# PE's order from a shorter figure for the tops' rows, expert weights stored by SyncE, and x1's low part one unit earlier, in a fused attention and expert kernel on one core

## What is computed

```python
masked = (qb >= kb) & (idx[None, :] - idx[:, None] - 2 * (kb - qb) >= 1)      # chunks of 64
scores = jnp.einsum('bqhd,bkhd->bhqk', q, k) * attn_scale[0]                  # 16 heads of 8
attn = jax.nn.softmax(jnp.where(mask[None, None], -jnp.inf, scores), axis=-1)
x = _layernorm(x + out @ Wo.T + bo)

scores = jax.nn.sigmoid(logits)                     # 32 experts in 8 groups, per token
# 4 best groups, in them 6 best experts, weights normed and times 2.5: combine[T, E]
for each expert: routed += combine[:, e] * ((silu(x @ g.T) * (x @ u.T)) @ dn.T)
shared_out = (silu(x @ shared_gate_w.T) * (x @ shared_up_w.T)) @ shared_down_w.T
x = _layernorm(x + routed + shared_out)
```

## Time and profile before

| | |
|---|---|
| time, median of 3 runs | 441.92 us (441.58 to 442.02) |
| profiled execution | 443.63 us, its span 441.6 us |
| PE busy | 411.4 us, 93% of the span |
| VectorE busy | 343.4 us, 78% |
| ScalarE busy | 226.8 us, 51% |
| GpSimd busy | 134.9 us, 31% |
| TensorE's granted clock, mean | 0.948 |

### The profile page before, as it was taken

One profiled execution on the slowest core, in us unless ns is written; L12 is line 12 of the kernel. 1 busy time (PEld: TensorE's weight loads), 2 busy tenths in 40 slices (PEclk: granted clock), 3 DMA queues, 4 the chain that ended last, 5 costly groups with the idle time before them and its releaser, 6 DMA issues.

```text
span 441.6 us, 8102 instructions
## 1 busy us (share of the span) xinstructions
PE 411.4 (93%) x2870; PEld 216.7 (49%) x2870; DVE 343.4 (78%) x775; ACT 226.8 (51%) x309; POOL 134.9 (31%) x257
## 2 busy tenths in 40 slices
PE   5659999999999999999989989999999999999993
PEld 2424434343333334334334446766776776666661
DVE  4969988898989898989954564976778768778863
ACT  4610077775778696877777784232432253332220
POOL 5000236685575666566554250000000000000000
PEclk9955579999999999999999998999999999999997
DMA  4565141120303012020000007333222233334430
GB/s 122 187 206 162 41 125 53 33 81 7 106 4 88 27 40 74 25 76 6 3 3 4 1 29 122 107 115 96 91 92 105 92 105 95 126 95 128 135 95 24
DMA packets 27391, 34.51 MB, mean 78 GB/s; under 512 B 5912, under 2 KB 16472, under 8 KB 27352
## 3 DMA queue, kind: packets, MB, share of 16 engines
q1 hardware_dynamic: 27016, 33.34, 25.6%
q10 hardware_dynamic: 336, 0.66, 0.5%
HBM read 29.33 MB, written 4.65 MB: 77 GB/s over the span
## 4 chain that ended last, share of the span: by engine, by line
PE 79%; DVE 13%; ACT 3%; issue 2%; DMA 1%; ACTq 1%; SPq 0%; POOL 0%; DVEq 0%; POOLq 0%
PE ps L1248 16%; PE ps L1350 13%; PE ps L1205 11%; DVE mx L907 10%; PE ps L1318 7%; PE ps L1320 7%; PE ps L1319 7%; PE ps L1229 7%; PE ps L1209 3%; ACT probs L805 2%; PE ps L1271 2%; PE ps L1283 1%; ACTq L542 1%; DMA bk<-in_bk 1%; PE ps L1171 1%
## 5 line engine op out<-in xcount | busy, mean ns | idle before, releaser
L907 DVE TENSOR_REDUCE mx<-ps 128x1 f32<-128x512 f32 (+3 forms) x304 | 179.5, 656 | 23.2 <-PE ps L1209 19.2
L805 ACT ACTIVATE probs<-ps 128x1024 f32<-128x1024 f32 (+2 forms) x160 | 143.4, 940 | 51.6 <-PE ps L1229 51.1
L1205 PE MATMUL ps<-rows_k,rows_q 48*128 48x512 bf16 (+3 forms) x384 | 103.0, 361 | 11.2 <-DMA rows_k<-scratch 7.1
L847 ACT ACTIVATE rows_q<-ps 128x512 f32<-128x512 f32 x68 | 40.6, 599 | 93.3 <-PE ps L1320 92.5
L1248 PE MATMUL ps<-probs,Vg 128*32 128x512 f32 (+3 forms) x768 | 82.5, 502 | 0.3 <-POOL probs L705 0.3
L1229 PE MATMUL ps<-rows_q,rows_k 51*128 51x512 bf16 (+3 forms) x384 | 71.5, 334 | 2.7 <-ACT probs L805 2.1
L1318 PE MATMUL ps<-x1hi,w_hi 128*128 128x512 f32 x136 | 73.9, 543 | 0.1
L1129 DVE TENSOR_TENSOR rows_k<-ps,rows_q 128x512 f32<-128x512 f32 x64 | 43.9, 686 | 34.5 <-PE ps L1350 34.1
L1205 PEld LDWEIGHTS ps<-rows_k,rows_q 48*128 48x128 bf16 x384 | 30.1, 96 | 80.8 <-DVE mx L907 65.0
L1350 PE MATMUL ps<-rows_q,w_down 128*128 128x512 f32 x136 | 69.7, 594 | 0.0
L701 POOL TENSOR_SCALAR_AFFINE_SELECT probs<-probs 64x512 f32<-64x512 f32 x64 | 42.3, 661 | 77.9 <-ACT probs L805 76.8
(11 more groups left out here) (107 smaller groups left out, 332.9 us busy)
## 6 DMA issues: line engine op xcount, KB each, us to landing
comb_rows<-weights SPq DMA_DIRECT2D x128, 128.0 KB, 3.0
scratch<-oT SPq DMA_DIRECT2D x8, 384.0 KB, 3.3
w_raw<-in_unitT SPq DMA_DIRECT2D x17, 128.0 KB, 2.4
rows_q<-scratch SPq DMA_DIRECT2D x16, 96.0 KB
rows_k<-scratch SPq DMA_DIRECT2D x14, 96.0 KB
w_down<-in_unitT SPq DMA_DIRECT2D x1, 1088.0 KB, 5.9
xT<-in_xT SPq DMA_DIRECT2D x4, 256.0 KB, 4.4
rows_q<-scratch SPq DMA_DIRECT2D x16, 64.0 KB
```

Source lines behind the costliest of these rows:

```text
L805: act.activation(dst, src, ACT.Exp).then_inc(exps_ready, 1)
L907: dve.tensor_reduce(dst, src, AX.X, ALU.max).then_inc(max_read, 1)
L1205: mm = pe.matmul(bank(max_bank(k), m, at), q, rows_k[r0:r0 + ROWS_QK, s, j * T + k0:j * T + k0 + m], start=True, stop=not first, tile_posi ...
```

## The change

Three edits.
1. The figure for the rows of a top in the planner goes from 6500 to 4700 ns. This alone changes `pe_order`, and with it `act_order` and `pool_order`.
2. The weights by expert: the planner's due time of ScalarE's copy loses 1500 ns, which puts the copy of the first chunk ahead of the last exponential in `act_order`. The store of each chunk (and the wait ahead of it) moves from ScalarE to SyncE, in front of the loads that read it.
3. VectorE's low part of x1 for the second quad stands behind unit 0 and not behind unit 1.

```diff
-    hop, rows_latency, load = 240, 6500, 7500
+    hop, rows_latency, load = 240, 4700, 7500
@@ attention_order
-                act_todo.append(("t", 0, i[k], t + hop + (1500 if kind == "comb" else 0), 500))
+                act_todo.append(("t", 0, i[k], t + hop, 500))
@@ SyncE's program
             for n in range(NC):
+                cols = slice(n * BANK, (n + 1) * BANK)
+                wait_step(sp, (n // 2, "comb", n % 2, 0))
+                sp.dma_start(a["weights"][:, cols], combT[:, cols]).then_inc(comb_stored[n], 16)
                 sp.wait_ge(comb_stored[n], 16)
@@ ScalarE's program, tail_step
                     act.copy(combT[:, cols], src[0:E, :]).then_inc(o, 1)
-                    act.wait_ge(o, count)
-                    act.dma_start(a["weights"][:, cols], combT[:, cols]).then_inc(comb_stored[n], 16)
@@ VectorE's program, the loop over units
-                if i == 1:
+                if i == 0:
                     x1_low((0, "x1T", 1, 0))
```

## The result

The changed kernel takes 443.64 us (median of 10 runs, 442.08 to 444.21) against 441.37 us (10 runs, 441.06 to 442.02) for the kernel before on the same chip. The ratio is 1.0042, with a 95% interval of 1.0029 to 1.0055: 0.4% slower. The prediction was 439.4 us and faster; it was wrong in the sign, and the time lies above its range. The profiled execution took 444.08 us, its span is 442.3.

The account below looks back on a forecast made before the run. The prediction took TensorE's time as the kernel's time, held up differently by stage. Its terms, -1.04 - 1.15 - 0.35 = -2.54 us off the median of 441.92, gave 439.4 us, with a range of 436.9 to 442.4.

Parts of the forecast that it names:

- part 1, pause: Ahead of the logits of x1's second quad: moving the low part removes TensorE's whole standstill, -1.04 us.
- part 1, low clock: At 269 to 273 us: without the standstill TensorE's clock no longer falls, -1.15 us, with 0 as other bound.
- part 2: Weights by expert: earlier copy on ScalarE, stores issued by SyncE, cost 0, up to +0.5 us if cover is gone.
- order, start: First scores come 1.3 us earlier and the clock rises as much earlier: -0.65 us (0 to -1.3).
- order, middle: Regular head groups: one more place where TensorE waits for a maximum, +0.1 us a group, +0.5 over five.
- order, end: Behind the last maximum: two score units and one value product fewer are left, -0.2 us.
- Part 1: x1's low part behind unit 0: TensorE's standstill and the low clock both go, -2.2 us together.
- rival D: End of attention: last maximum later, VectorE's chain holds TensorE before the transposes, clock falls; +1.4 us, 443.3, chance 0.12.
- Rival E: x1's low part finds its high part late, the standstill only moves; -0.35 us is left, 441.6, chance 0.05.
- rival C: Middle: new order loses 0.5 us in each of five groups, +2.5; -0.54 in all, 441.4, chance 0.13.

Follow-up runs that it names:

- before_a: The kernel before, unchanged, run and profiled a second time: 441.03 us, ratio 0.9999.
- e1: The kernel before with the third edit only (x1's low part behind unit 0): 440.94 us, ratio 0.9998 to the kernel before.
- e3: The changed kernel with the planner's figure back at 6500, so the second and third edits without the new order: 441.04 us, ratio 0.9997 to the kernel before.
- after: The changed kernel with all three edits, first measurement and profile: 443.64 us, ratio 1.0042 to the kernel before.
- after_a: The changed kernel, unchanged, run and profiled a second time: 443.55 us, ratio 1.0054 to the kernel before.
- e2: The kernel before with the planner's figure alone changed (4700 for 6500): 444.34 us, ratio 1.0073 to the kernel before.
- e4: The changed kernel with runs of three maximum entries ahead of a score unit broken up on TensorE from group 1 on: 443.82 us, ratio 1.006.
- e14: The changed kernel with the last maximum entry of full stretches moved behind the next value product, if that had room: 441.10 us, ratio 0.9979 to the kernel before.
- e10: The changed kernel with the planner's latency between engines at 200 ns in place of 240: 437.64 us, ratio 0.990 to the kernel before.
- e8: The changed kernel with figure 6500 and the planner's lead cut from 1.5 to 1.2 groups: 442.89 us, ratio 1.0018 to the kernel before.
- e15: The changed kernel with planner latency 200 ns and the last maximum entry of full stretches moved behind the next value product: 437.75 us, ratio 0.991.

## Why the prediction was wrong, step by step

| step | predicted, us | shown, us | by |
|---|---|---|---|
| part 1, pause | -1.04 | 0 | before_a, e1 |
| part 1, low clock | -1.15 | 0 | before_a, e1 |
| part 2 | 0 | 0 | e3 |
| order, start | -0.65 | -0.9, -0.5 or +1.0, as the clock rises early or late | after, after_a; e2 and e4 |
| order, middle | +0.5 | +3.2 (4 x 0.81) | e2, e3 |
| order, end | -0.2 | -0.9 | e2, e4, after_a |

**Part 1** failed at its first number, the 1.04 us. The mechanism of the pause is right: the changed kernel shows every step of it, and e4's trace has the late load without the pause. That the pause brought the low clock is not shown (see rival D). But the earlier trace rows showed a load that landed 1.2 us late in that execution. The profiled execution lay 1.71 us above the median, and the prediction noted that and then took the full 2.19 us off the median. Had it asked what made that execution slower, the pause and the low clock would have been the first suspects. The bound of 0, which was given, was the value. The low clock was also sized too small for that execution: from the first logit to unit 4 before_a took 3.27 us (268.10 to 271.37), so 4.84 was 1.57 too much and not 1.15. With the pause that is 2.6 of the 2.7 us by which the first profile was longer. Rival E had this size; its reason (a late high part) was wrong. The Trainium skill (DMA: Bandwidth & Descriptors, "Latency and other measured facts") gives HBM's access latency as 0.2 us on average and 2 us at high load; a spread of 1.2 us between two executions fits in there, and would have been a warning. Whether load on HBM did it, no run shows.

**Part 2** was right in its sum, 0 (e3). Two of its premises hold in e3 alone: there ScalarE's copy stands ahead of the last exponential, and the loads behind the store begin 2.65 us ahead of x1's transposes, 0.7 more than the 1.9 of the kernel before. In the changed kernel the copy stays behind the exponentials, and the loads begin 2.17 us ahead, as in e2 without the edit (2.16). The prediction walked the planner and missed this.

**The start** went as said in the changed kernel's profile, but not in every execution. The first scores, at 54.13 in the earlier trace rows, came at 53.03. The clock rose in the slice 58 to 59 and not 61 to 62:

```profile
58.00:59.00 1.00, 1.00 (x12) 0.24 (x10) 0.00 (x0) 0.00 (x0) 0.85 (x3) 0.77 0.34 117
```

From the first maximum to the last of group 3 the changed kernel took 98.35 us, the one before 99.25; in after_a it was 98.80. But in e2 and e4, with the same start of the list, the clock rose only at about 65 us, and the same stretch took 100.3. Counted from the first maximum the rise came at 33.7 to 34.8 us in the four traces of the old list and at 30.7 to 37.2 in these four of the new one. So the start's term has no one value, and its range (0 to -1.3) is left on the upper side by two of four traces. The 10 times of the changed kernel fall in two heaps, 442.1 to 442.5 and 443.6 to 444.2; that these are the two places of the rise, or the fall named next, is likely but not shown.

**The middle** is the step that decided the sign. The prediction saw the mechanism (each engine waits for the other, rival C) and sized it at 0.1 us a group, with 0.5 as its bound. It counted runs of three side by side, which e4 showed to cost nothing. It didn't count entries between two value products, which its own lists had for group 3: the fourth behind v2.10 is easy to read off. By e14 these crowded stretches account for 0.46 of the 0.81 us; the rest stays open. The bound also rested on TensorE's idle time of 0.7 us a group, as if that limited what could be lost or gained. But the idle time hardly moved; the busy time did, by +0.63 us in the new list and by -0.61 in e10. Four groups, 4 to 7, took 0.81 more each and not five; group 3 got 0.4 shorter (25.87 for 26.31). That lies in the start's -0.9, with -1.2 in group 1 and +0.7 in group 2.

**The end** gave more than predicted. From the last maximum to x1's transposes the kernel before took 37.4 us, after_a and e2 36.5: 0.9 us less, about one exponential (0.81). Which link of the chain behind the last maximum got shorter, no run singles out.

**Rival D** named the right sign and nearly the right time (443.3), but its mechanism is not there: the transposes L1290 stand directly behind a value product, and TensorE didn't wait for L971. The clock did fall in the first tail of the changed kernel's profile, at another place. TensorE stood 1.28 us ahead of the first tail step, and a microsecond later, in the slice 232 to 233, the clock fell. Order of time on TensorE and the next slice, changed kernel:

```profile
231.29 0.63 PE L1272 MATMUL ps<-ident,oT 128*128 128x128 f32 x4 [1.28 <-ACT mn L815]
```
```profile
233.00:234.00 1.00, 1.00 (x6) 0.28 (x3) 0.00 (x0) 0.31 (x1) 0.86 (x4) 0.50 0.03 8
```

The same kernel in after_a, with the same wait and no fall:

```profile
230.93 0.63 PE L1272 MATMUL ps<-ident,oT 128*128 128x128 f32 x4 [1.28 <-ACT mn L815]
```
```profile
233.00:234.00 1.00, 1.00 (x12) 0.73 (x11) 0.47 (x2) 0.28 (x1) 0.92 (x3) 1.00 0.00 0
```

The fall cost the first of the two some 1.5 us (38.0 us from the last maximum to the transposes, 36.5 without it). e14's profile has the same wait of 1.28 us and the fall behind it (0.52 in the slice 231 to 232), e2's and e8's have the wait and no fall. And the clock fell once where TensorE had hardly paused at all: e15, in which it stood for no more than 0.23 us at a time from 85 us on, has a granted clock of 0.72 in the slice 103 to 104 and of 0.50 in the next.

So a pause of this size is neither enough for a fall nor needed for one, and what brings it stays open. The Trainium skill (TensorE: Matmul & The Clock Gate, "HAM oscillation — how this bites in real kernels") ties falls to longer gaps; the falls behind 1.04 and 1.28 us and the one behind 0.23 us don't agree with that.

Put together: 0 for parts 1 and 2, and for the order -0.9 + 3.2 - 0.9 = +1.4 with the earliest rise of the clock, +1.0 + 3.2 - 0.9 = +3.3 with the latest, and 1.5 more where the clock falls in the tail. Measured: +2.3 between the medians, +3.2 for e2.

## What to carry to other kernels

A wait in a single profile is a sample: before taking it off the median, look at a second profile, or ask what the profiled execution has that the median has not. In a fixed program order with a small ring between two engines, count what stands between the long steps that don't feed the ring as well as what stands side by side: here three banks bore three entries per stretch, the fourth waited, and the consumer had run dry just before. Take the count as a hint and not as a price, since it didn't rank the lists tried here. An engine's idle time doesn't bound what another order of the same work can gain or lose. A planner's figure is a seed for a list as much as a model: 40 ns on one latency moved the period by 1.3 us, so try several and measure the period of one group.

## What the runs showed of the hardware

The same 64-partition load of rows took 3.0 us to land in one execution of the kernel before and 4.2 in another, at the same place. The granted clock rose at 58 to 65 us with one and the same list on TensorE (the changed kernel and e2), while TensorE was busy for 24.5 of 25 us. It fell in some executions behind pauses of 1.04 and 1.28 us, in others not, and once behind pauses of 0.23 us at most. The same matmuls of a group kept TensorE busy for 23.76 us in e10, 24.37 in the kernel before and 25.00 in the changed one. As a share of the time that is 97% each time: the busy share doesn't tell how well neighbours overlap. What sets that difference (24.59 to 25.44 at nearly the same place of the scores) stays open.
